# Interleaving two row groups of a split-precision graph layer and reordering the two engines that prepare its operands

## The reference

```python
def reference(x, adj, W, b):                      # x 4096x256, adj 4096x4096, W 256x256, b 256, all fp32
    h = jnp.maximum(_layernorm(x, axis=-1), 0.0)  # rows: (x - mean) / sqrt(var + 1e-5)
    agg = jnp.matmul(adj, h)
    out = jnp.matmul(agg, W.T) + b
    return x + jax.nn.relu(out)
```

## Time and profile before

| | |
|---|---|
| median of 3 runs | 381.09 us (380.98 to 381.16) |
| profiled execution, its own time | 380.8 us |
| its span, first to last instruction | 379.0 us |
| PE busy | 375.1 us (99%), 1651 matmuls |
| PE weight load, DVE, ACT, POOL busy | 308.1, 212.2, 181.8, 50.1 us |
| granted TensorE clock | 1.0 throughout |

### The profile page before, as it was taken

One profiled execution on the slowest core, in us unless ns is written; L12 is line 12 of the kernel. 1 busy time (PEld: TensorE's weight loads), 2 busy tenths in 40 slices (PEclk: granted clock), 3 DMA queues, 4 the chain that ended last, 5 costly groups with the idle time before them and its releaser, 6 DMA issues.

```text
span 379.0 us, 4516 instructions
## 1 busy us (share of the span) xinstructions
PE 375.1 (99%) x1651; PEld 308.1 (81%) x1651; DVE 212.2 (56%) x294; ACT 181.8 (48%) x228; POOL 50.1 (13%) x88
## 2 busy tenths in 40 slices
PE   8999999999999999999999999999999999999997
PEld 4888888888888888888888888888888888888885
DVE  5999988874744453535564544444464444444424
ACT  5888776764443434343643343433355243434341
POOL 5687732320010000000001000000000100000000
PEclk9999999999999999999999999999999999999999
DMA  7989877577659565655566856565656775555203
GB/s 263 369 301 304 275 256 258 185 235 256 210 186 317 174 215 178 208 177 209 176 206 207 294 178 209 178 205 184 201 189 195 256 242 195 187 202 185 92 2 111
DMA packets 22774, 80.25 MB, mean 212 GB/s; under 512 B 2496, under 2 KB 2880, under 8 KB 22752
## 3 DMA queue, kind: packets, MB, share of 16 engines
q1 hardware_dynamic: 19584, 68.30, 54.1%
q0 software_dynamic: 3168, 11.67, 8.6%
HBM read 75.76 MB, written 4.19 MB: 211 GB/s over the span
## 4 chain that ended last, share of the span: by engine, by line
PE 98%; DMA 1%; DVE 0%; ACT 0%; POOL 0%; issue 0%; POOLq 0%
PE bank L421 92%; PE bank L463 6%; DMA x_sb<-x_dram 1%; ACT adj_hi L346 0%; POOL rstd L204 0%; ACT h_sb L352 0%; DVE out_sb L320 0%; DVE stats L240 0%; DVE mean_var L245 0%; DVE var_eps L249 0%; POOLq L200 0%
## 5 line engine op out<-in xcount | busy, mean ns | idle before, releaser
L421 PE MATMUL bank<-adj_hi,h_sb 128*128 128x512 f32 x1024 | 254.3, 389 | 0.2 <-ACT adj_hi L346 0.2
L229 DVE TENSOR_TENSOR adj_lo<-adj_in,adj_hi 128x1024 fp32r<-128x1024 f32 x126 | 154.6, 1227 | 145.7 <-ACT adj_hi L342 145.5
L421 PEld LDWEIGHTS bank<-adj_hi,h_sb 128*128 128x128 f32 x1024 | 192.0, 188 | 40.5 <-issue 0.5
L342 ACT ACTIVATE adj_hi<-adj_in 128x1024 fp32r<-128x1024 f32 x126 | 133.5, 1060 | 176.7 <-PE bank L421 174.5
L421 PE MATMUL bank<-adj_lo,h_sb 128*128 128x512 f32 x512 | 137.5, 389 | 0.0
L421 PEld LDWEIGHTS bank<-adj_lo,h_sb 128*128 128x128 f32 x512 | 96.1, 188 | 20.0
L204 POOL TENSOR_TENSOR rstd<-var_eps,minus_half 128x1 f32<-128x1 f32 x32 | 30.5, 954 | 3.4 <-DVE var_eps L249 0.8
L221 POOL DMA_DIRECT2D out_t_dram<-out_sb x3 | 2.2, 726 | 211.0 <-DVE out_sb L320 211.0
L352 ACT ACTIVATE h_sb<-centred,rstd 128x256 fp32r<-128x256 f32 x32 | 16.0, 499 | 3.6 <-POOL rstd L204 3.2
L362 ACT ACTIVATE centred<-x_sb,neg_mean 128x256 f32<-128x256 f32 x31 | 15.5, 500 | 2.1 <-DVE neg_mean L264 1.9
L270 DVE SCALAR_TENSOR_TENSOR h_sb<-centred,rstd,h_sb 128x256 fp32r<-128x256 f32 x32 | 15.3, 477 | 1.0 <-ACT h_sb L352 1.0
(11 more groups left out here) (25 smaller groups left out, 42.7 us busy)
## 6 DMA issues: line engine op xcount, KB each, us to landing
adj_in<-adj_t_dram SPq DMA_DIRECT2D x126, 512.0 KB, 3.6
xt_sb<-x_t_dram POOLq DMA_DIRECT2D x4, 1024.0 KB, 7.4
x_sb<-x_dram POOLq DMA_DIRECT2D x7, 512.0 KB, 6.5
out_t_dram<-out_sb POOLq DMA_DIRECT2D x3, 1024.0 KB, 4.9
adj_in<-adj_t_dram SPq DMA_DIRECT2D x4, 256.0 KB, 4.8
out_t_dram<-out_sb SPq DMA_DIRECT2D x3, 256.0 KB, 2.0
x_sb<-x_dram POOLq DMA_DIRECT2D x3, 128.0 KB, 4.6
w_sb<-w_t_dram POOLq DMA_DIRECT2D x1, 256.0 KB, 6.0
```

Source lines behind the costliest of these rows:

```text
L229: nc.vector.tensor_tensor(adj_lo[:, k, :], adj_in[:, k, :], adj_hi[:, k, :].bitcast(fp32), ALU.subtract).then_inc(s_lo, 1)
L342: nc.scalar.activation(adj_hi[:, k, :], adj_in[:, k, :], ACT.Copy).then_inc(s_hi, 1)
L421: last = nc.tensor.matmul(bank(g, kb, c)[:], h_sb[:, t, hp, kb * P:(kb + 1) * P], adj_parts[ap][:, n % U, chunk(c)], start=(t == 0 and (hp ...
```

## The change

`UNITS` now lists the units in the order in which all engines take them: tiles 0 to 23 of h, each for group 0 and then for group 1; then tiles 24 to 31 of group 0; then tiles 24 to 31 of group 1; then groups 2 and 3 as before. So tile t of h is first used in unit 2t. What follows a group is placed 4 and 8 units behind its last unit (60 and 64 for group 0, 68 and 72 for group 1).

In VectorE's stream, for n from 2 to 32, the order becomes `adj_rest(n)`, `h_rest(n - 1)`, `moments(n)`, `minus_mean(n)`; in ScalarE's `adj_rounded(n)`, `centre(n - 1)`, `h_rounded(n - 1)`. h is still made at one tile per unit, through unit 32. The first chunk of adj is rounded by VectorE instead of ScalarE. GpSimd's queue issues tile 1 of x at the start, and tiles 2, 3 and 4 to 7 behind the first root. TensorE takes the passes of the first two units in another order by chunks, runs two short matmuls of constants instead of three, and waits for W's split at unit 60 instead of 32. The last five stores count on one semaphore, with one wait instead of five.

```diff
+    UNITS = [(g, t) for t in range(TILES - LAG) for g in range(2)]
+    UNITS += [(g, t) for g in range(2) for t in range(TILES - LAG, TILES)]
+    UNITS += [(g, t) for g in range(2, GROUPS) for t in range(TILES)]
...
-            for i in range(1, U):
-                load_x(pool, i)
+            load_x(pool, 1)
...
                 if t == 0:
-                    load_x(pool, U)
+                    for i in range(2, U + 1):
+                        load_x(pool, i)
...
+            def first_rounded():
+
+                dve.wait_ge(s_early[0][0], 16)
+                nc.vector.tensor_copy(adj_hi[:, 0, chunk(0)], adj_in[:, 0, chunk(0)]).then_inc(s_hi, 1)
...
             moments(0)
             first_var_eps()
             centre_first()
+            first_rounded()
             h_rest(0)
+            early_rest(0, 0)
+            early_rest(0, 1)
             moments(1)
             minus_mean(1)
-            early_rest(0, 0)
-            early_rest(0, 1)
-            moments(2)
-            minus_mean(2)
-            h_rest(1)
             early_rest(1, 0)
             early_rest(1, 1)
-            moments(3)
-            minus_mean(3)
-            adj_rest(2)
-            h_rest(2)
-            for t in range(3, TILES):
-                if t + 1 < TILES:
-                    moments(t + 1)
-                    minus_mean(t + 1)
-                adj_rest(t)
-                h_rest(t)
+
+            for n in range(EARLY, TILES + 1):
+                adj_rest(n)
+                h_rest(n - 1)
+                if n < TILES:
+                    moments(n)
+                    minus_mean(n)
...
             h_rounded(0)
-            early_rounded(0, 0)
+
+            act.wait_ge(s_hi, 1)
             early_rounded(0, 1)
+            early_rounded(1, 0)
             centre(1)
-            early_rounded(1, 0)
-            h_rounded(1)
             early_rounded(1, 1)
-            for t in range(EARLY, TILES):
-                centre(t)
-                adj_rounded(t)
-                h_rounded(t)
+            for n in range(EARLY, TILES + 1):
+                adj_rounded(n)
+                if n > EARLY:
+                    centre(n - 1)
+                h_rounded(n - 1)
...
-            for s in s_last:
-                sp.wait_ge(s, 16)
+            sp.wait_ge(s_last, 16 * len(pieces(LAST)))
```

More of the change, by code:

```diff
@@ L37, in bass_preln_gnn_residual @@
     WARM_UP = 10
-    WARM_ON = 3
+    WARM_ON = 2
     EARLY = 2
+    LAG = 8
     SPLIT_AT = 4
     OUT_AT = 8
+    UNITS = [(g, t) for t in range(TILES - LAG) for g in range(2)]
+    UNITS += [(g, t) for g in range(2) for t in range(TILES - LAG, TILES)]
+    UNITS += [(g, t) for g in range(2, GROUPS) for t in range(TILES)]
     X_PIECES = [(t, t + 1) for t in range(4)] + [(t, t + 4) for t in range(4, TILES, 4)]
@@ L114, in bass_preln_gnn_residual @@
         s_out = sem("out_stored")
-        s_last = [sem(f"out_stored_last{i}") for i in range(SUMS + 1)]
+        s_last = sem("last_group_stored")
         block = ctx.enter_context(nc.Block())
@@ L128, in x_piece, with end_of, made_chunk, made_unit @@
             return next(i for i, (a, b) in enumerate(X_PIECES) if a <= t < b)
-        def made_chunk(t, c):
-            return CHUNKS * t + c + 1
-        def made_tile(n):
+        def end_of(g):
+            return max(n for n, u in enumerate(UNITS) if u[0] == g) + 1
+        SPLIT = {end_of(g) + SPLIT_AT: g for g in range(LAST)}
+        OUT = {end_of(g) + OUT_AT: g for g in range(LAST)}
+        def made_chunk(n, c):
+            return CHUNKS * n + c + 1
+        def made_unit(n):
             return made_chunk(n, CHUNKS - 1) if n < EARLY else CHUNKS * EARLY + n - EARLY + 1
@@ L157, in _, with load_chunk @@
         def _(sp):
-            def load_chunk(t, c):
-                sp.dma_start(adj_in[:, t, chunk(c)], adj_v[:, t, chunk(c)]).then_inc(s_early[t][c], 16)
+            def load_chunk(n, c):
+                g, t = UNITS[n]
+                at = g * GW + c * BANK
+                sp.dma_start(adj_in[:, n, chunk(c)], adj_v[:, t, at:at + BANK]).then_inc(s_early[n][c], 16)
             def load_adj(n):
-                g, t = divmod(n, TILES)
+                g, t = UNITS[n]
                 if n >= U:
-                    sp.wait_ge(s_hi, made_tile(n - U))
-                    sp.wait_ge(s_lo, made_tile(n - U))
+                    sp.wait_ge(s_hi, made_unit(n - U))
+                    sp.wait_ge(s_lo, made_unit(n - U))
                 sp.dma_start(adj_in[:, n % U, :], adj_v[:, t, g * GW:(g + 1) * GW]).then_inc(s_adj[n % U], 16)
@@ L173, in _ @@
             load_chunk(1, 1)
-            for n in range(EARLY, GROUPS * TILES):
+            for n in range(EARLY, len(UNITS)):
                 load_adj(n)
@@ L180, in _ @@
                 at = LAST * GW + c * BANK
-                sp.dma_start(out_v[:, o, at + a:at + b], out_sb[:, o, within(c, a, b)]).then_inc(s_last[i], 16)
-            for s in s_last:
-                sp.wait_ge(s, 16)
+                sp.dma_start(out_v[:, o, at + a:at + b], out_sb[:, o, within(c, a, b)]).then_inc(s_last, 16)
+            sp.wait_ge(s_last, 16 * len(pieces(LAST)))
         @block.gpsimd
         def _(pool):
-            for i in range(1, U):
-                load_x(pool, i)
+            load_x(pool, 1)
             nc.gpsimd.memset(minus_half[:], -0.5).then_inc(s_const, 1)
@@ L227, in adj_rest, with early_rest @@
                 k = n % U
-                dve.wait_ge(s_hi, made_tile(n))
+                dve.wait_ge(s_hi, made_unit(n))
                 nc.vector.tensor_tensor(adj_lo[:, k, :], adj_in[:, k, :], adj_hi[:, k, :].bitcast(fp32),
                                         ALU.subtract).then_inc(s_lo, 1)
[L232 to L235, removed]
+            def first_rounded():
+                dve.wait_ge(s_early[0][0], 16)
+                nc.vector.tensor_copy(adj_hi[:, 0, chunk(0)], adj_in[:, 0, chunk(0)]).then_inc(s_hi, 1)
+            def early_rest(n, c):
+                dve.wait_ge(s_hi, made_chunk(n, c))
+                nc.vector.tensor_tensor(adj_lo[:, n, chunk(c)], adj_in[:, n, chunk(c)],
+                                        adj_hi[:, n, chunk(c)].bitcast(fp32), ALU.subtract).then_inc(s_lo, 1)
             def moments(t):
@@ L322, in make_out @@
                                                    op0=ALU.max, op1=ALU.add).then_inc(s_sum, 1)
[L324 to L330, removed]
+            for n in range(TILES + 1, len(UNITS)):
+                if n in SPLIT:
+                    sums_rest(SPLIT[n])
+                if n in OUT:
+                    make_out(OUT[n])
+                adj_rest(n)
             sums_rest(LAST)
@@ L342, in adj_rounded, with early_rounded @@
                 nc.scalar.activation(adj_hi[:, k, :], adj_in[:, k, :], ACT.Copy).then_inc(s_hi, 1)
-            def early_rounded(t, c):
-                act.wait_ge(s_early[t][c], 16)
-                nc.scalar.activation(adj_hi[:, t, chunk(c)], adj_in[:, t, chunk(c)], ACT.Copy).then_inc(s_hi, 1)
+            def early_rounded(n, c):
+                act.wait_ge(s_early[n][c], 16)
+                nc.scalar.activation(adj_hi[:, n, chunk(c)], adj_in[:, n, chunk(c)], ACT.Copy).then_inc(s_hi, 1)
             def h_rounded(t):
@@ L385, in sums_rounded @@
                 if g < LAST:
-                    act.wait_ge(s_pe, (g + 1) * TILES)
+                    act.wait_ge(s_pe, end_of(g))
                 for i, (c, kb) in enumerate(GROUP_BANKS):
@@ L400, in _ @@
             act.wait_ge(s_b, 16)
[L401 to L407, removed]
+            for n in range(TILES + 1, len(UNITS)):
+                if n in SPLIT:
+                    sums_rounded(SPLIT[n])
+                if n in OUT:
+                    add_bias(OUT[n])
+                adj_rounded(n)
             add_bias(LAST)
@@ L415, in _, with add_up @@
             adj_parts = (adj_hi, adj_lo)
-            def add_up(g, t, chunks, hp, ap):
-                n = g * TILES + t
+            def add_up(n, chunks, hp, ap):
+                g, t = UNITS[n]
                 for kb in range(KB):
@@ L425, in add_up, with early_unit, sum_unit @@
                 return last
[L427 to L442, removed]
+            def early_unit(n):
+                pe.wait_ge(s_hhi, 1)
+                pe.wait_ge(s_hi, made_chunk(n, 0))
+                add_up(n, [0], 0, 0)
+                pe.wait_ge(s_hlo, 1)
+                add_up(n, [0], 1, 0)
+                pe.wait_ge(s_hi, made_chunk(n, 1))
+                add_up(n, [1], 0, 0)
+                pe.wait_ge(s_lo, made_chunk(n, 0))
+                add_up(n, [0], 0, 1)
+                add_up(n, [1], 1, 0)
+                pe.wait_ge(s_lo, made_chunk(n, 1))
+                add_up(n, [1], 0, 1).then_inc(s_pe, 1)
+            def sum_unit(n, chunks, arrived):
+                g, t = UNITS[n]
                 for hp, ap in PASSES:
@@ L446, in sum_tile @@
                             if g == 0:
-                                pe.wait_ge(s_hhi, n + 1)
```

(22 more changed lines are left out.)

## The result

The changed kernel took 399.91 us in the median of 5 runs (399.7 to 400.85), the kernel before, on the same chip, 380.98 (380.78 to 381.16): a ratio of 1.0498, 95% interval 1.0486 to 1.0509. It is 5% slower, 18.9 us, near the forecast of 399.1 and inside its range. The profiled execution has a span of 398.0 us against 379.0.

What follows compares the result with a forecast made beforehand. TensorE, busy 99%, bounds the kernel; the new loop's turn of 3.34 us exceeds its 2.72 over 29 turns, delaying unit 34 by 18.3 us: 380.8 + 18.3 = 399.1 us, range 395.5 to 404.5.

Steps and rivals of the forecast that it cites:

- rival 3: In TensorE's units: gaps of 0.6 us each make the granted clock fall, a unit takes 5.44, tens of microseconds; 3%.
- rival 1: In the loop: port held longer, or epsilon (L198) caught too; turn 3.61 us, 7.8 more, 406.9 if always; 15%.
- roughly cancel: At the start: x tiles 2 and 3 leave the queue, 4 to 7 move closer; third adj piece stays at 9.72, ±0.5 us.
- rival 2: In the loop: the root escapes L229, taking 0.55; turn at least 2.49 us, under 2.72, time 380.6; 8%.

## Why the prediction was right

**The mechanism.** The loop through root, `h_rounded` and `h_rest` is shown from three sides. The wait put on the root's side shortened the 29 roots of the stage to 0.55 us and gave back 7.7 us; leaving out the root gave back everything; moving the moments or `h_rest` by one turn gave back the 5% but for 0.4 us at most. Against rival 3, the granted clock stayed at 1.00 in the whole stage. The long root was argued from the earlier trace rows and is now shown to be L229's doing.

**The turn, term by term** (forecast, then measured between 59.64 and 65.53): L245 to L229 0.28, 0.29; L229 1.24, 1.24; to the root's end 0.41, 0.40; to `h_rounded` 0.03, 0.04; `h_rounded` 0.50, 0.51; to `h_rest` 0.03, 0.04; to L240 0.40, 0.40; to L245 0.45, 0.45. Forecast 3.34, measured 3.37. The hundredths by which the terms were low make 0.9 us in 29 turns. The mean of 3.39 has 0.5 us more from two longer turns. In one epsilon was caught (1.29 us at 32.65, behind the issue of the loads of W on GpSimd's queue), and L246 started 3.64 us behind the one before: that is rival 1, in one turn of 29, at nearly its price of 3.61. In the other (3.59) VectorE stood 0.26 us ahead of `minus_mean` for a reason the trace does not show; the root then started only 0.02 us behind L246 and took 1.60.

**Where it starts and ends.** L229 of unit 3 was to end at 14.32 and ended at 13.65. The third piece of adj was taken at 9.05 instead of 9.72, so the later pieces of x did not "roughly cancel" as forecast. The other traces agree, with a wide spread: with these loads of x the third piece was taken between 9.01 and 9.67 (eight traces), with those of before between 9.32 and 10.82 (five). That x left the queue free for adj is the likely reason, and no run shows it alone. L229 of unit 32 was to end at 111.18 and ended at 111.94; TensorE was to start unit 34 at 116.86 and started at 117.62 (116.71 plus four matmuls). Less 98.51 of before, this is a delay of 19.1 us, and the span grew by 19.0. So there was no further stall, and nothing was given back, as forecast. The two errors, -0.7 at the start and +1.4 in the turns, had opposite signs, so that the total came within 0.8 us is in part luck.

**The port.** The root ends 0.40 us behind L229 whether it starts 0.24 (1.40 long), 0.08 (1.54 long) or 0.02 (1.60 long) behind L229's start. The Trainium skill's rule ("SBUF — State Buffer", "Who interferes with whom") names the pair that collides; its "fully blocks" would put the whole 0.55 us behind L229, and the total near 403. The rows decide for 0.40, and nearer 400. Nor does the other side of the rule show: where the root began first, L229 was no longer than elsewhere (1.23 us).

**The other edits.** The copy of the first chunk took 0.47 us (0.63 had been taken), the first matmul stood at 5.43 in the profiled run, 0.41 us earlier than before where -0.2 to +0.6 had been said, and unit 2 at 11.25 instead of 11.45. Both are lost in the loop, as forecast. The semaphore is worth nothing that can be measured.

**What was said wrong.** I expected the line of PE to fall under 9 tenths. TensorE lost 19.0 us, but only 6.8 of them are idle time in the record (398.0 - 387.3 against 379.0 - 375.1); the other 12.2 are booked as busy. One turn shows how:

```profile
61.23 1.19 PE L437 MATMUL bank<-adj_lo,h_sb 128*128 128x512 f32 x4 [0.28 <-DVE adj_lo L246]
...
62.26 2.12 PE L437 MATMUL bank<-adj_hi,h_sb 128*128 128x512 f32 x8
...
64.59 1.20 PE L437 MATMUL bank<-adj_lo,h_sb 128*128 128x512 f32 x4 [0.21 <-DVE adj_lo L246]
```

Of the 3.36 us from 61.23 to 64.59, 3.15 count as busy, 0.43 more than a unit takes. The four matmuls behind the gap are recorded in 1.19 us, where four without a gap take 1.07, and the next eight in 2.12 instead of 1.98. The remaining 0.17 us come from the record itself: a matmul is recorded 0.39 us long and the next starts 0.2267 behind it, so ahead of a gap the last one reaches that much further. The loss is plain in the weight loads, which wait 29 times for adj_lo.

The least turn of rival 2, 2.49 us, left out L229. If L229 starts 0.20 behind the root as in the earlier trace rows, the turn is 0.53 + 0.20 + 1.16 + 0.85 = 2.74 us, no shorter than TensorE's 2.72. No run shows whether such a rhythm would have held.

And the first reading of the kernel before with only VectorE's order moved was wrong by nearly 14 us or more, since I had looked for the loop in the root alone and not in ScalarE's queue.

**Is there a version that beats both?** None was found. The two that open the loop measure 0.9993 and 0.9992, both intervals reaching just beyond no change. They are clear of the changed kernel by 5% and not clear of the one before. With TensorE busy 99%, the interleaving had a fraction of a microsecond to win.

## What to carry to other kernels

When an instruction is moved in an in-order stream, write down the loop it closes over all engines, one hand-over after the other, and compare its length with the period of the engine that sets the pace; an engine's busy share says nothing of it, and here VectorE is busy 68% of the stage of h (12 to 110 us) in the slower kernel, and was busy 85% between 12 and 100 us in the faster one. A result that comes from another engine wants a whole turn between its cause and its use: moving either end of that span by one turn was worth 5% here. And a small instruction on GpSimd that started beside VectorE's long subtraction ended only behind it, so a wait that kept them apart was worth more than it cost.

## What the runs showed of the hardware

GpSimd's power of one column took 0.55 us alone. If it starts while a VectorE subtraction with two SBUF inputs runs (128x1024, 1.24 us), it ends 0.40 us behind it, so it lasted 1.40, 1.54 or 1.60 us by when it began; if it starts first, neither is delayed (0.55 and 1.23). A VectorE copy of 128x512 from fp32 to fp32r took 0.47 us; the subtraction of that size took 0.69 and ScalarE's copy 0.63. Weight loads that waited 0.7 us in each of 29 units, over 98 us, left the granted clock at 1.0 (2.4 GHz), and so did turns of 3.94 us, with 1.2 us lost in each, in the kernel before with only VectorE's order moved.
